# Constant matmuls into an unread bank ahead of TensorE's waits in a graph block on one core

## The reference

```python
xn = _layernorm(x)
# two graph layers
h0 = prelu(xn @ lin_W.T + lin_b)
for l in range(2):
    h = h0 + segment_sum(h0[src], dst)
    h = prelu(h @ W1[l].T + b1[l]) @ W2[l].T + b2[l]
    h0 = relu(batchnorm(h))
# attention with softmax(q) over features, softmax(k) over nodes
mix = layernorm((softmax(q) @ (softmax(k).T @ v)) @ w_out + b_out)
x = x + h0 + mix
# feed-forward, gate g averaged over the nodes
y = _layernorm(x)
g = mean(relu(y @ gfc1.T + b) @ gfc2.T + b)
W1m, W2m, b1m, b2m = W + sum_e g[e] * tv[e]
x = x + layernorm(y + relu(y @ W1m.T + b1m) @ W2m.T + b2m)
```

## Time and profile before

| | us |
|---|---|
| median of 3 runs | 511.06 (510.05 to 512.14) |
| the profiled execution | 510.37 |
| its span, first to last instruction | 508.6 |
| PE busy in it | 470.0 |
| DVE, ACT, POOL busy in it | 324.8, 250.3, 166.1 |

### The profile page before, as it was taken

One profiled execution on the slowest core, in us unless ns is written; L12 is line 12 of the kernel. 1 busy time (PEld: TensorE's weight loads), 2 busy tenths in 40 slices (PEclk: granted clock), 3 DMA queues, 4 the chain that ended last, 5 costly groups with the idle time before them and its releaser, 6 DMA issues.

```text
span 508.6 us, 9887 instructions
## 1 busy us (share of the span) xinstructions
PE 470.0 (92%) x3564; PEld 358.0 (70%) x3564; DVE 324.8 (64%) x749; ACT 250.3 (49%) x524; POOL 166.1 (33%) x176
## 2 busy tenths in 40 slices
PE   1989999999999998999999997999999879989892
PEld 1768567886765676666999984679998768956641
DVE  4766698747999846754655358634333675439687
ACT  4787354147712354254344755424346477724454
POOL 1369243111095003033326880003323023304403
PEclk9999999999999989999999999999999959989998
DMA  8700102202020002002100001000000394000014
GB/s 241 210 3 18 66 0 85 84 1 84 0 85 0 2 3 84 0 14 79 77 0 0 1 6 57 1 0 1 0 6 0 124 411 210 1 0 2 1 54 148
DMA packets 5246, 27.44 MB, mean 54 GB/s; under 512 B 1036, under 2 KB 1161, under 8 KB 3544
## 3 DMA queue, kind: packets, MB, share of 16 engines
q1 hardware_dynamic: 5208, 26.92, 15.4%
HBM read 24.36 MB, written 2.56 MB: 53 GB/s over the span
## 4 chain that ended last, share of the span: by engine, by line
PE 75%; DVE 14%; ACT 5%; issue 3%; POOL 1%; DMA 1%; SPq 0%; DVEq 0%; ACTq 0%
PE ps L459 46%; PE ps L631 17%; PE ps L448 4%; PE ps L725 3%; PE ps L524 2%; PE ps L534 1%; PE ps L445 1%; DVE r L1665 1%; DVE late L1168 1%; DVE r L1167 1%; DVE r L1677 1%; POOL late L1718 1%; DVE ohs L1158 1%; DVE r L1655 1%; DMA x<-in_x 1%
## 5 line engine op out<-in xcount | busy, mean ns | idle before, releaser
L459 PE MATMUL ps<-r,wslot 128*128 128x250 f16 x840 | 98.1, 277 | 4.4 <-DVE r L1167 4.3
L459 PEld LDWEIGHTS ps<-r,wslot 128*128 128x128 f16 x840 | 83.0, 100 | 16.8 <-DVE r L1167 5.8
L631 PE MATMUL ps<-late,r 125*128 (+1 forms) x800 | 87.1, 269 | 0.9 <-DVE r L1387 0.9
L1726 POOL TENSOR_TENSOR wslot<-stage,wslot 128x512 f16<-128x512 f32 x32 | 39.5, 1266 | 139.6 <-ACT wslot L777 139.6
L631 PEld LDWEIGHTS ps<-late,r 125*128 125x128 f16 x800 | 77.4, 97 | 10.8 <-issue 1.6
L459 PE MATMUL ps<-wslot,r 128*125 128x512 f16 x300 | 69.4, 381 | 0.0
L459 PE MATMUL ps<-wslot,late 128*125 128x512 f16 x240 | 54.9, 380 | 3.1 <-DVE late L1459 2.7
L459 PEld LDWEIGHTS ps<-wslot,r 128*125 128x125 f16 (+1 forms) x300 | 39.3, 136 | 22.4 <-issue 2.3
L1754 POOL TENSOR_TENSOR late<-ohs,late 128x250 f16<-128x250 f32 x40 | 25.6, 651 | 88.8 <-ACT late L953 88.8
L459 PE MATMUL ps<-late,wslot 128*128 (+1 forms) x480 | 51.7, 269 | 0.0
L459 PEld LDWEIGHTS ps<-late,wslot 128*128 128x128 f16 x480 | 46.5, 97 | 5.3 <-issue 0.8
(11 more groups left out here) (183 smaller groups left out, 732.3 us busy)
## 6 DMA issues: line engine op xcount, KB each, us to landing
late<-in_tv SPq DMA_DIRECT2D x2, 4096.0 KB, 17.3
x<-in_x SPq DMA_DIRECT2D x5, 448.0 KB
out<-r SPq DMA_DIRECT2D x10, 224.0 KB
stage<-in_w_up SPq DMA_DIRECT2D x2, 1024.0 KB, 5.5
stage<-in_w_down SPq DMA_DIRECT2D x2, 1024.0 KB, 5.3
stage<-in_w_lin SPq DMA_DIRECT2D x1, 1024.0 KB, 6.4
stage<-in_w_k SPq DMA_DIRECT2D x1, 1024.0 KB, 4.8
stage<-in_w_q SPq DMA_DIRECT2D x1, 1024.0 KB, 4.7
```

Of the source, the lines that this page charges most:

```text
L459: last = nc.tensor.matmul(out, stat_(hs, b), mov(hm, b), start=start and n == 0, stop=stop and n == 3 * blocks - 1)
L631: last = nc.tensor.matmul(bank("t", m), u_nat[layer][:, p, h, m * 128:(m + 1) * 128], counts(h)[:, chunk], start=(start and h == 0 and p = ...
L1726: last = nc.gpsimd.tensor_tensor(wslot[:, i % SLOTS, 1, k, :], stage[:, k * D:(k + 1) * D], wslot[:, i % SLOTS, 0, k, :], ALU.subtract)
```

## The change

A function `keep_busy(bank_, n)` is added. It issues n matmuls of the constants `ident` and `ones` into a bank that nothing reads before it is written anew. It is called ahead of TensorE's waits: at the start behind `consts` (27), before the first and the fourth chunk of `lin` (7 and 18), before the blocks 0, 2 and 3 of the second layer's first tile (4, 9, 7), before the blocks 2 and 3 of the first gnn tile (11, 7), before the first x2 flips (14), before `g_ready` (11), before the first merge (3) and before ffn2 (10): 128 in all, at twelve places. For three of them a wait is set ahead: `wait_done(pe, "x", "rows", 2)` is new before the x2 flips, `wait_done(pe, "y", "gnn", T)` moves from the merge to before `g_ready`, and the wait for `b2_ready` comes before the one for `wm_split`.

```diff
                 def ready(b):
                     if t % 2 == 0:
+                        if layer and t == 0:
+                            keep_busy(7, (4, 0, 9, 7)[b])
                         pe.wait_ge(in_low, KB * (J * layer + t // 2) + b + 1)
...
+            def keep_busy(bank_, n):
+
+                for _ in range(n):
+                    nc.tensor.matmul(ps[:, bank_, 0:128], ident[:, :], ones[:, :], start=True, stop=True)
+
             pe.wait_ge(consts, 1)
+            keep_busy(7, 27)
...
             flip_pair(0)
             for j in range(J):
+                keep_busy(7, {0: 7, J - 2: 18}.get(j, 0))
                 wait_done(pe, "x", "xn", 2 * j + 2)
...
             def flip_gnn(g):
 
                 for t in (2 * g, 2 * g + 1):
-                    flip_tile_to_nat("y", "gnn", gnn_t, t, lambda m: pe.wait_ge(layer_out, KB * (g - 1) + m + 1) if g else
-                                     pe.wait_ge(first_out, m + 1))
+
+                    def ready(m):
+                        if t == 0:
+                            keep_busy(7, (0, 0, 11, 7)[m])
+                        if g:
+                            pe.wait_ge(layer_out, KB * (g - 1) + m + 1)
+                        else:
+                            pe.wait_ge(first_out, m + 1)
+
+                    flip_tile_to_nat("y", "gnn", gnn_t, t, ready)
...
             flip_gnn(0)
             flip_gnn(1)
+            wait_done(pe, "x", "rows", 2)
+            keep_busy(5, 14)
             flip_x2(0)
...
+            wait_done(pe, "y", "gnn", T)
+            keep_busy(7, 11)
             pe.wait_ge(g_ready, 1)
...
             pe.wait_ge(got_tv, 32)
-            wait_done(pe, "y", "gnn", T)
+            keep_busy(7, 3)
             merge_w1(6, 0)
...
+            pe.wait_ge(b2_ready, 2)
+            keep_busy(7, 10)
             pe.wait_ge(wm_split, FB + 2)
-            pe.wait_ge(b2_ready, 2)
             natural("ffn2", hid_t, w2m, blocks=FB, ready=lambda i: pe.wait_ge(tmp_free, KB + 2 * KB * J + J + i + 1),
```

## The result

| | before | after |
|---|---|---|
| median, us | 510.31 (17 runs, 509.1 to 512.16) | 513.13 (17 runs, 511.81 to 513.84) |
| the profiled execution | 510.37 | 513.2 |
| its span | 508.6 | 511.4 |
| mean granted clock | 0.975 | 0.991 |

The ratio of the times is 1.0054, with a 95% interval of 1.0042 to 1.0067: the change makes the kernel 2.8 us slower. The forecast was 510.9, no measurable change. 513.13 lies inside its range (506.0 to 513.5), near the upper end, but on the other side of the bound of 0.5%.

A forecast was written before the change was run, and what follows sets the result against it. TensorE was taken to bound the kernel (75% of the chain). Six terms, -0.5 - 0.1 + 1.0 - 0.1 - 1.1 + 0.6 = -0.2, gave 510.9 us against the median of 511.06; range 506.0 to 513.5.

The forecast's parts named there:

- the start: 27 and 7 dummies around the first transposes: end at 9.4, 0.5 late, repaid by faster transposes; -0.5, from -0.5 to +1.0.
- The gate: 11 and 3 dummies behind the gate: +0.8 late, then the merge in 3.45 instead of 5.37; -1.1 in all.
- ffn2: 10 dummies in the wait before ffn2: +0.6, with no clock fall there to cure.
- rival (a): Dummies cost half or hide in latencies, so nothing is late: -5.0, 506.1 us; chance 0.22, in full or part.
- The fourth chunk: 18 dummies before it start its matmuls 1.5 late, but the clock stays up: loss and cure cancel, -0.1.
- the prediction's own +1.5: The fourth chunk's term if there is no clock fall there to cure.
- The second layer: 4, 9 and 7 dummies at its first tile delay the blocks, nothing comes back: +1.0, from 0 to +1.1.
- The flips: Dummies at gnn and x2 flips: about 1.0 late, repaid by full clock, chain gets little; -0.1, from -1.0 to +1.0.
- Rival (b): The 14 dummies before the x2 flips meet a low clock and take 6.0 us: 515.2 us; chance 0.07.
- Rival (c): Late starts aren't repaid, without the falls at 36 and 452: +3.3, 514.4 us; chance 0.09.
- (d): VectorE and ScalarE keep more gains or absorb more delays: 1.5 either way, 509.4 to 512.4; chance 0.62 together with the forecast.
- The forecast's own part of it: The forecast together with another share for the other engines: 508.5 to 512.6 us, chance 0.62.

The follow-up runs named there:

- e1_start: The changed kernel with only the 27 and 7 dummies at the start, other counts 0: 514.82 us, ratio 1.0085 to before.
- f4_start_tiny: The changed kernel with only the start's 27 and 7 dummies, plus 16 one-column float32 matmuls as padding: 510.97 us, ratio 1.001 to before.
- f1_start_fit: The changed kernel with the start cut to 15 and 5 dummies, plus 14 one-column float32 matmuls as padding: 510.0 us, ratio 1.0001 to before.
- e3: The changed kernel with only the 4, 9 and 7 dummies at the second layer's first tile: 510.75 us, ratio 1.0004 to before.
- e5: The changed kernel with only the 11, 7 and 14 dummies at the gnn and x2 flips, with the wait for the rows: 511.07 us, ratio 1.0027.
- e4: The changed kernel with only the 10 dummies before ffn2, the bias wait ahead of the weight's: 511.46 us, ratio 1.0013 to before.
- e6: The changed kernel with only the 11 and 3 dummies behind the gate, with the moved wait: 509.89 us, ratio 0.9999 to before.
- e2_chunk4: The changed kernel with only the 18 dummies before the fourth chunk, other counts 0: 514.11 us, ratio 1.0071 to before.

## Why the prediction was wrong, step by step

**The step that failed is the start.** It was the term of the sum that was mis-sized: forecast at -0.5, it measured +0.8 in the profile of the changed kernel and of e1_start, and +1.4 in that of f4_start_tiny. Two of its inputs were wrong. The dummies were to begin at 1.7, when the constants are ready; they begin at 2.94. And the clock was to rise at about 5.3; it rises at 7.1 here, and at 6.0 to 9.0 over the nine profiles, which no single count can fit. "End at 9.4, 0.5 late" became an end at 11.0, 2.1 late, and the faster transposes and first chunk made good only 1.3. The upper bound that I gave (+1.0, dummies that end at 11.2) was close to it and I took the other end: the late bound was argued from a clock that rises at 8.8, and I had not asked when TensorE can issue its first instruction. f1_start_fit shows what the surplus of 12 and 2 dummies costs, 2.3 to 3.1 us. With +0.8 in the place of -0.5 the forecast's own sum would have been +1.1, 512.2.

**Smaller terms erred the same way.** The gate was to win 1.1 and wins 0.65: the merge takes 3.60 instead of 3.45, and it starts 1.1 later than the kernel's lateness of 2.6 would have it (455.67 against 451.94), where 0.8 was forecast. ffn2 costs 0.85 instead of 0.6. Together with the start's 1.3 that makes 2.0 of the 3.0 between the forecast's -0.2 and the account's +2.8. Most of the rest is the 0.85 between 42 and 305, of which e3 to e5 show 0.3 to 0.5 without any edit there; what made the other half isn't known, and the profiled pair is only two executions. That the medians differ by 2.8 as well isn't accounted for by the profiles in full: the one-place medians (f4 +0.10%, e3 +0.04%, e4 +0.13%, e5 +0.27%, e6 -0.01%) sum to 0.53% beside the 0.54% measured, but each is uncertain by 0.2% or more, f4's has the missing fall at 36 in it, and the fourth chunk has no clean run of its own, so that the agreement is no proof.

**What was right.** The price of a dummy: two records, 0.107 each, 0.215 a pair, which refutes rival (a), in which it costs half; no wait was left behind the dummies. The fourth chunk, where loss and cure cancel against the kernel before (-0.15 against -0.1), though e1_start and f4_start_tiny have no fall there to cure, in which case the prediction's own +1.5 holds. The second layer (+1.1 against +1.0). The flips, where the cure of 10 us at half clock gives the chain nothing: x2's flips come at 417.16, 4.2 later than before, of which 2.6 are the kernel's lateness, and from 423 on nothing has been lost or won. Rival (b), dummies at half clock there, didn't come: 28 records in 3.29. There the transposes keep the full clock with the dummies among them; the Trainium skill (TensorE: Matmul & The Clock Gate, Part 4: PE-mode transpose) says that they don't count as work for the clock, which neither profile contradicts, since in the changed kernel matmuls always stand between them. Rival (c), late starts that nothing repays, is what came about in kind, though not where it was put: the fall at 452 was cured and paid back 0.65, that at 36 was gone, whether by the 18 dummies or by the start's, and the start and the second layer went unrepaid. (d), another share for the other engines, isn't needed for the account: behind the second layer's tile, the merge and ffn2 the lateness is passed on whole, and at the flips it is absorbed as forecast.

**The range** took in the result by luck. The forecast's own part of it ended at 512.6, below 513.13; the rest up to 513.5 was there for the mild end of rival (c). The chances were too sure of the sum: all six terms rested on the moment at which dummies end, and in three of them (start, gate, ffn2) they ended later than I had worked out. I had treated these errors as independent, and they weren't.

## What to carry to other kernels

Filler work ahead of a wait pays only where it ends before the value is there: count it at the measured price (two records for a float32 matmul), from the moment at which the engine issues its first instruction, at half clock until the profile shows the rise, and round down, the more so at the start, where the rise itself moved by 3 us between profiles; here 55 dummies gain 0.5%, and 0.8% with the standstill padded away, where 128 lose 0.5%. Try whether a place needs its own dummies once an earlier one has them: the fourth chunk didn't in the two profiles that can tell. A clock that reads full is no gain in itself: each cured stretch has to be weighed against how late its first matmul starts. And when one place of a change is tried alone, look in the profile for standstills far from the edit before the time is believed: here two such runs came out 4 us above the kernel before, most of it for a reason far from their place.

## What the runs showed of the hardware

- In the profiles of six kernels with 72 to 136 instructions added ahead of a branch, TensorE is idle for 1.9 to 3.3 us at its entry, 1.4 to 3.0 of it put down to issue; in twelve with none or with 200 and more it is idle there for 0.9 to 1.5, the wait for VectorE. The clock can be at half for 3.3 us behind it (e1_start, e2_chunk4).
- Increments of a semaphore in TensorE's stream aren't free: 0.05 us each where 3 or 4 stand between products (60: 3.1, 80: 3.8), 0.1 each where 6 or 10 do (120: 11.4, 200: 20.3), falls of the clock included.
- The first dummy runs at 2.94 in all nine profiles that have dummies at the start, 1.2 us after the constants are ready. Until the first change of level the clock column reads 1.00, though the pace of the records is half.
- The level rises between 6.0 and 9.0 in these nine (7.1 in the changed kernel, 6.1 in f1_start_fit, 8.5 in f4_start_tiny), behind the same first dummy at 2.94.
- Which of its waits the clock falls behind changes from one profile to the next (e1_start has falls at 164 and 239 and none at 36 or 186, e2_chunk4 has them at 187, 238 and 313, the kernel before at 36 and 186), and for the kernel before alone the mean granted clock lies between 0.971 and 0.984 from one execution to another.
